# A mixture-of-experts kernel with seven-product blocks: the first groups reordered on ACT, PE and POOL

## The reference

```python
x = x + L0(x, probs, shared_gate)      # x: 16 x 256 tokens x 256, D = 256, F = 1024, f32

def L0(h, gating_probs, shared_gate_prob, Wg, Wu, Wd, Sg, Su, Sd):
    g = jnp.einsum('bsd,edf->ebsf', h, Wg)              # 8 experts
    u = jnp.einsum('bsd,edf->ebsf', h, Wu)
    expert_outs = jnp.einsum('ebsf,efd->ebsd', jax.nn.silu(g) * u, Wd)
    expert_output = jnp.einsum('be,ebsd->bsd', gating_probs, expert_outs)
    shared = jnp.einsum('bsf,fd->bsd', jax.nn.silu(h @ Sg) * (h @ Su), Sd)
    sg = shared_gate_prob[:, :, None]
    return (1.0 - sg) * expert_output + sg * shared
```

## Time and profile before

| | us |
|---|---|
| median of 3 runs | 2124.58 (2123.74 to 2124.72) |
| profiled execution, its own time | 2123.92 |
| its span, first to last instruction | 2122.1 |

### The profile page before, as it was taken

How to read it: one execution, slowest core, us unless ns; L and a number is a source line. 1 busy time by engine, 2 the same in 40 slices (tenths; PEclk the granted TensorE clock), 3 DMA queues, 4 the chain that set the end, 5 groups by cost and what they waited for, 6 DMA issues and landing times.

```text
span 2122.1 us, 33959 instructions
## 1 busy us (share of the span) xinstructions
PE 2098.0 (99%) x9180; PEld 1717.0 (81%) x9180; DVE 1452.6 (68%) x2640; ACT 1303.7 (61%) x2336; POOL 1609.4 (76%) x1435
## 2 busy tenths in 40 slices
PE   7999999999999999999999999999999999999998
PEld 5888888888788888888878888888887888888886
DVE  6666666666666666666676666666667666666666
ACT  6777777777556555555555655555555555555554
POOL 7988777878388777777778877777777777777776
PEclk9999999999999999999999999999999999999999
DMA  8776767666555455455445555445445555544543
GB/s 297 243 250 224 253 225 249 227 241 225 191 208 208 177 206 199 173 198 208 176 188 204 189 200 207 177 187 208 189 177 206 185 201 206 202 173 196 208 180 117
DMA packets 122455, 433.78 MB, mean 204 GB/s; under 512 B 13728, under 2 KB 41504, under 8 KB 122400
## 3 DMA queue, kind: packets, MB, share of 16 engines
q1 hardware_dynamic: 122400, 433.19, 54.5%
HBM read 329.85 MB, written 103.28 MB: 204 GB/s over the span
## 4 chain that ended last, share of the span: by engine, by line
PE 97%; DVE 1%; issue 0%; DMA 0%; POOL 0%; ACT 0%; SPq 0%; DVEq 0%; ACTq 0%; POOLq 0%
PE chain_ps L549 15%; PE chain_ps L551 14%; PE chain_ps L550 14%; PE down_ps L551 8%; PE down_ps L549 8%; PE down_ps L550 8%; PE p_ps L549 6%; PE p_ps L551 6%; PE p_ps L550 6%; PE side_ps L549 4%; PE side_ps L550 4%; PE side_ps L551 4%; DVE acc L972 1%; DMA w_raw<-w 0%; DVE h_forms L975 0%
## 5 line engine op out<-in xcount | busy, mean ns | idle before, releaser
L386 POOL TENSOR_TENSOR h_forms<-h_t,h_forms 128x512 fp32r<-128x512 f32 x432 | 564.3, 1325 | 274.2 <-ACT h_forms L858 274.2
L549 PE MATMUL chain_ps<-x_hi,gate_forms 128*128 128x512 f32 x1080 | 423.9, 393 | 2.2 <-DVE p_ps L972 1.1
L551 PE MATMUL chain_ps<-x_hi,gate_forms 128*128 128x512 f32 x1080 | 421.1, 390 | 0.0
L550 PE MATMUL chain_ps<-x_lo,gate_forms 128*128 128x512 f32 x1080 | 420.8, 390 | 0.0
L386 POOL TENSOR_TENSOR h_t<-h_b,h_t 128x512 f32<-128x512 f32 x214 | 312.6, 1461 | 78.9 <-DVE h_b L966 63.6
L972 DVE TENSOR_TENSOR p_ps<-tap_p,chain_ps 128x512 f32<-128x512 f32 x216 | 150.3, 696 | 251.5 <-PE chain_ps L551 251.5
L875 ACT COPY chain_ps<-chain_ps 128x512 f32<-128x512 f32 x216 | 123.1, 570 | 289.3 <-DVE h_a L966 201.3
L858 ACT CAST h_forms<-h_t 128x512 fp32r<-128x512 f32 x432 | 268.9, 623 | 14.9 <-DVE h_t L975 2.2
L386 POOL TENSOR_TENSOR w_lo<-w_raw,w_hi 128x1152 fp32r<-128x1152 f32 x71 | 190.5, 2683 | 85.7 <-ACT w_hi L775 84.8
L549 PEld LDWEIGHTS chain_ps<-x_hi,gate_forms 128*128 128x128 f32 x1080 | 202.5, 188 | 60.9 <-ACT chain_ps L875 8.1
L551 PEld LDWEIGHTS chain_ps<-x_hi,gate_forms 128*128 128x128 f32 x1080 | 202.7, 188 | 43.4
(11 more groups left out here) (105 smaller groups left out, 4882.2 us busy)
## 6 DMA issues: line engine op xcount, KB each, us to landing
...
```

Of the source, the lines that this page charges most:

```text
L386: return nc.gpsimd.tensor_tensor(dst, a, b, ALU.subtract)
L549: nc.tensor.matmul(bank, w_high, hi, start=start, stop=False, **on)
L550: nc.tensor.matmul(bank, w_high, lo, start=False, stop=False, **on)
L551: return nc.tensor.matmul(bank, w_low, hi, start=False, stop=stop, **on)
```

## The change

Four things. (1) ACT: in the first two units its work stands in the order in which it is needed; tap_p1(0) comes after the third x form. In units 2 to 7 it makes the high parts of chunks 3, 4, 5, 6 (and 7 behind the silus), 8, 9, and the down high parts of pairs 0, 1, 2, 3, 4 in units 2, 3, 5, 6, 7. (2) PE: in units 0 and 1 the plain products stand ahead of chained ones, and P4(0) behind P1 and P5 of chunk 1. (3) The second chunk's forms are made in parts on ACT and POOL, and POOL has a written order for its first eight units (`first_chunks`); keep(0), (2), (4), (6) of SP wait for the down sums too, since these now may come after the low parts. (4) The x forms of the next group start eight units later (OPENING_DELAY), and a fourth expert is written out on ACT and POOL. On DVE the low part of A11, A12 moves ahead of the sums, the x low parts are reordered, and gate0, gate1 of chunk 0 stand ahead of the last x low part.

```diff
@@ -29,6 +29,13 @@
 X_HI_AT = {6: B11, 8: T1, 10: B21, 12: T2, 14: B22, 16: T3, 18: T4}
 X_LO_AT = {10: B11, 12: T1, 14: B21, 16: T2, 18: B22, 20: T3, 22: T4}
 X_EXPERTS = 3
+OPENING_EXPERTS = 4
+OPENING_DELAY = 8
+
+HI_IN_UNIT = {2: 3, 3: 4, 4: 5, 5: 6, 6: 8, 7: 9}
+HI_BEHIND_UNIT = {5: 7}
+DOWN_HI_IN_UNIT = {2: 0, 3: 1, 5: 2, 6: 3, 7: 4}
+FIRST_X_HI = (B11, T1, B21, B22, T2, T3, T4)
 SUM_OF = {T1: 0, T2: 1, T3: 2, T4: 3}
 
 H_AT = {B11: 0, T1: 2, B22: 4, B21: 6, T2: 8, T3: 10, T4: 12}
...
@@ -263,6 +272,8 @@
             def keep(e, k):
                 n = group(0, e, k)
                 s, j = k % SLOTS, k // 2
+                if isinstance(n, int) and n in (0, 2, 4, 6):
+                    sp.wait_ge(d_sums, 4 * (j + 1))
                 if k % 2 == 1:
                     sp.wait_ge(d_lo_done, e * PAIRS + j + 1)
                 elif isinstance(n, int) and n == 0:
...
@@ -448,33 +459,71 @@
                 pool.wait_ge(x_hi_done, X_FORMS * g + form + 1)
                 subtract(x_lo[:, g % 2, form], x_source(g, form), x_hi[:, g % 2, form].bitcast(F32)).then_inc(x_lo_done, 1)
 
-            def next_x(g, e, k):
-                at = e * CHUNKS + k
+            def next_x(g, e, k, delay=0):
+                at = e * CHUNKS + k - delay
                 if g + 1 < GROUPS and at in X_SUM_AT:
                     x_form(g + 1, X_SUM_AT[at])
                 if g + 1 < GROUPS and at in X_LO_AT:
                     x_form_lo(g + 1, X_LO_AT[at])
 
...
+            def next_sums(e, k):
                 n = group(0, e, k)
                 s = (k + 1) % SLOTS
                 if not isinstance(n, int) or n < PER - 1:
                     uses = e * (CHUNKS // SLOTS) + (k + 1) // SLOTS + 1
                     pool.wait_ge(w_loaded[s], 16 * uses)
                     weight_sums(n + 1, s)
+
+            def pair_sums(e, k):
+                n = group(0, e, k)
+                uses = e * (CHUNKS // SLOTS) + k // SLOTS + 1
+                pool.wait_ge(d_loaded[k % SLOTS], 16 * uses)
+                pool.wait_ge(d_loaded[(k + 1) % SLOTS], 16 * uses)
+                if not isinstance(n, int) or n >= 4:
+                    pool.wait_ge(d_hi_done, e * PAIRS + k // 2 - 1)
+                down_sums(e * PAIRS + k // 2, k // 2)
+
+            def prepare(e, k):
+                next_sums(e, k)
                 if k % 2 == 0:
-                    uses = e * (CHUNKS // SLOTS) + k // SLOTS + 1
-                    pool.wait_ge(d_loaded[k % SLOTS], 16 * uses)
-                    pool.wait_ge(d_loaded[s], 16 * uses)
-                    if not isinstance(n, int) or n >= 4:
-                        pool.wait_ge(d_hi_done, e * PAIRS + k // 2 - 1)
-                    down_sums(e * PAIRS + k // 2, k // 2)
-                if not isinstance(n, int) or n > 0:
-                    weight_lo(e, k)
+                    pair_sums(e, k)
+                weight_lo(e, k)
                 if k % 2 == 1:
                     down_lo(e, k // 2)
-                if isinstance(e, int) and e < X_EXPERTS:
-                    next_x(0, e, k)
+                if isinstance(e, int) and e < OPENING_EXPERTS:
+                    next_x(0, e, k, OPENING_DELAY)
+
+            def second_lo(first, last):
+                return subtract(lo_of(1, first, last), raw_of(1, first, last), hi_of(1, first, last).bitcast(F32))
+
+            def first_chunks():
+
+                next_sums(0, 0)
+                pool.wait_ge(w1_hi_done, 1)
+                second_lo(A11, A12).then_inc(w1_lo_done, 1)
+                pool.wait_ge(w_hi_done, 1)
+                second_lo(S3, S4).then_inc(w1_lo_done, 1)
+                next_sums(0, 1)
+                pool.wait_ge(w_hi_done, 2)
+                second_lo(D0, D1).then_inc(w_lo_done, 1)
+                weight_lo(0, 2)
+                pair_sums(0, 0)
+                next_sums(0, 2)
+                down_lo(0, 0)
+                weight_lo(0, 3)
+                next_sums(0, 3)
+                pair_sums(0, 2)
+                weight_lo(0, 4)
+                down_lo(0, 1)
+                next_sums(0, 4)
+                pair_sums(0, 4)
+                next_sums(0, 5)
+                weight_lo(0, 5)
+                next_sums(0, 6)
+                down_lo(0, 2)
+                pair_sums(0, 6)
+                weight_lo(0, 6)
+                prepare(0, 7)
 
...
@@ -517,10 +566,11 @@
                     next_x(g, e, 2 * j + 1)
                 form_lo_of(T1, 5, pc + 1)
 
-            for e in range(X_EXPERTS):
+            first_chunks()
+            for e in range(1, OPENING_EXPERTS):
                 for k in range(CHUNKS):
                     prepare(e, k)
-            with pool.Fori(X_EXPERTS, EXPERTS - 1) as e:
+            with pool.Fori(OPENING_EXPERTS, EXPERTS - 1) as e:
                 for k in range(CHUNKS):
                     prepare(e, k)
             for k in range(CHUNKS):
...
+            def p1_of(n, k):
+                s = k % SLOTS
                 opening = isinstance(n, int) and n == 0
-                if not opening:
-                    p4(0, (k - 1) % CHUNKS, n - 1, first=isinstance(n, int) and n == 1)
                 if opening:
                     first_w(0)
+                elif isinstance(n, int) and n == 1:
+                    pe.wait_ge(w1_lo_done, 1)
                 else:
                     pe.wait_ge(w_lo_done, n)
                 after(pe, h_lo_done[0], n - 1)
-                product(chain, made(s, A11), x_of(0, B11, opening), start=True, stop=True).then_inc(p1_done, 1)
+                product(chain_ps[:, k % 2, :], made(s, A11), x_of(0, B11, opening), start=True, stop=True).then_inc(p1_done, 1)
+
...
+            def p6_of(n, k):
                 pe.wait_ge(p1_tapped, n + 1)
-                product(chain, made(s, S2), x_of(0, T2, opening), start=False, stop=True, goes_on=True).then_inc(p6_done, 1)
+                opening = isinstance(n, int) and n == 0
+                product(
+                    chain_ps[:, k % 2, :], made(k % SLOTS, S2), x_of(0, T2, opening), start=False, stop=True, goes_on=True
+                ).then_inc(p6_done, 1)
+
...
+            def first_units():
+
+                p1_of(0, 0)
+                p5_of(0, 0)
+                p2_of(0, 0)
+                p6_of(0, 0)
+                p3_of(0, 0)
+                p7_of(0, 0)
+                p1_of(1, 1)
+                p5_of(1, 1)
+                p4(0, 0, 0, first=True)
+                p6_of(1, 1)
+                p3_of(1, 1)
+                p2_of(1, 1)
+                p7_of(1, 1)
+                pe.wait_ge(h_lo_done[1], 1)
+                first_w(3)
+                down1(0, start=True, stop=False)
+
+            def unit(e, k):
+
+                n = group(0, e, k)
+                p4(0, (k - 1) % CHUNKS, n - 1)
+                p1_of(n, k)
+                p5_of(n, k)
+                pe.wait_ge(h_lo_done[0], n - 1)
+                down0((k - 2) % CHUNKS, start=isinstance(n, int) and n == 2, stop=False)
+                p6_of(n, k)
+                p2_of(n, k)
+                p3_of(n, k)
+                p7_of(n, k)
+                pe.wait_ge(h_lo_done[1], n)
+                down1((k - 1) % CHUNKS, start=False, stop=False)
 
             Q_OF = {1: (DA11, B11), 2: (DA12, B21), 3: (DS4, B22), 4: (DA22, T4), 5: (DS1, T1), 6: (DS2, T2), 7: (DS3, T3)}
             SUM_BANK = {2: q2_ps, 3: q3_ps, 4: q4_ps, 5: q5_ps}
...
-            for k in range(CHUNKS):
+            first_units()
+            for k in range(2, CHUNKS):
                 unit(0, k)
             with pe.Fori(1, EXPERTS) as e:
...
+            def silu_of(t, n):
+                act.wait_ge((gate0_done, gate1_done)[t], n + 1)
+                after(act, (h0_done, h1_done)[t], n)
+                nc.scalar.activation(silu[:, t], gate[:, t], ACT.Silu).then_inc(silu_done[t], 1)
+
+            def unit(e, k):
+                n = group(0, e, k)
+                early = isinstance(n, int) and n < CHUNKS
+                if early:
+                    chunk, behind, down_pair = HI_IN_UNIT[n], HI_BEHIND_UNIT.get(n), DOWN_HI_IN_UNIT.get(n)
+                    chunk = divmod(chunk, CHUNKS)
+                    down_pair = None if down_pair is None else divmod(down_pair, PAIRS)
+                else:
+                    chunk, behind = ahead_of(e, k), None
+                    if isinstance(n, int) and n + AHEAD >= PER:
+                        chunk = None
+                    down_pair = (chunk[0], chunk[1] // 2) if chunk and k % 2 == 1 else None
+
+                h1_hi_of(n - 1)
+                tap1(n, k)
+                tap5(n)
+                h0_hi_of(n - 1, k - 1)
+                if chunk:
+                    weight_hi(*chunk, 0)
+                tap_u2_of(n, k)
+                if chunk:
+                    weight_hi(*chunk, 1)
+                    if down_pair:
+                        down_hi(*down_pair)
+                if isinstance(e, int) and e < OPENING_EXPERTS:
+                    next_x(0, e, k, OPENING_DELAY)
```

(89 more changed lines are left out.)

80 lines of the change are left out of this document (28 added, 52 removed).

## The result

Over 20 runs each, the changed kernel takes 2127.66 us (median, 2124.9 to 2129.07), the kernel before 2124.36 us (2122.96 to 2126.68). The ratio is 1.0015 with an interval of 1.0008 to 1.0021: some 3 us slower, inside the 0.2% that the prediction called no change, and 1.6 us above the 2126.1 that it named. The profiled execution of the changed kernel has a span of 2124.6 us and took 2126.7 us.

A forecast was written before the change was run, and what follows sets the result against it. PE is busy 99% of the span, so only its idle time or slow-clock matmuls can be won. Opening gain 5.5 less loop loss 7.0 gives 1.5 us later: 2126.1 us, range 2125.4 to 2127.8, chance 0.58.

The forecast's parts named there:

- The opening: Up to P1 of chunk 2: the new order starts P1(2) at 24.0 instead of 29.52, a gain of 5.5 us.
- The POOL loops: Chunks 3 to 6: PE waits for POOL's w_lo, which waits on ACT's high parts; a loss of 7.0 us.
- the one behind chunk 6: After P1(6): no further stall, PE keeps 7.48 us a unit, the shift of 1.5 us stands to the end.
- (D): Opening wins less, through DVE contention 1 us and a late clock rise: 2127.1 to 2128.1 us; chance 0.13.
- (B): PE keeps the opening's whole gain because POOL leads by 3 to 5 us: 5.5 us faster, 2119.1; chance 0.10.
- (A): Loops cost less, chunk 6's loss is gone: 2.1 us faster, 2122.5; chance 0.13.
- (C): POOL's own steps lengthen in the loops beside DVE, from 13% more (2.8 us): 2128.9 us; chance 0.06.
- Edits at nothing: SP's later keeps and loads, longer ACT and POOL programs (0 to 0.3 us), second_lo in pieces: taken as no cost.
- the rule weighed: DVE and POOL contend for SBUF: x_lo of B22 and w_lo of S3, A22 could be charged 0.5 us in all.

The follow-up runs named there:

- e1: The changed kernel with ACT making the high parts of down pair 2 in unit 4 instead of unit 5; ratio to before 0.9990.
- e5: The changed kernel with only POOL's order in units 2 to 7 rewritten, same steps, each w_lo ahead of the d_lo; ratio to before 0.9979.
- e4: The changed kernel with 12 filler matmuls on PE in its pause ahead of P1 of chunk 6, output the same; ratio to before 1.0005.
- e6: The kernel before with only the x forms eight units later and a fourth expert written out; median 2124.04 us against 2124.24, ratio 0.9999.
- e9: e5 with SP's loads of w(n+4) ahead of the d form stores in the first eight chunks; median 2118.06 us, ratio to before 0.9971.

## Why the prediction was right, and where it was short

**The opening.** P1(0) 5.2 (5.25 measured), P5(0) 8.1 (8.23), P6(0) 11.1 (10.93), P1(2) 24.0 (23.66). The two pauses of PE before P2(1) and P4(1), 0.85 and 1.3 us, came as 1.0 and 0.9. The waits before these two ended with the steps named, DVE's h1_lo and up1. In between, errors cancelled: up1(0) came 0.6 us earlier than summed (14.82 for 15.4) and the coefficients behind it took 1.23 us for the 0.84, where the range had allowed for 0.17. The clock rose at 12.3, taken as 12.4; that this is so near is luck, since in the other traces with PE's same opening it rose between 11.2 and 12.9. P1(2) lay between 23.35 and 23.66 in all of them, so the reading that the moment hardly matters held.

**The POOL loops.** Chunk 3: loss 1.6, measured 1.68 (32.82 - 23.66 = 9.16 for 7.48). Chunk 4: 0, measured 0.17. Chunk 5: 1.8, measured 1.72. Chunk 6: 3.6, measured 3.55 (11.03 for 7.48). Sum 7.0, measured 7.1. P1(6) was put at 61.0 and came at 60.70, the waits of PE at 1.6, 1.7 and 3.5 and came as 1.5, 1.5 and 3.3. POOL idle for d_hi, 2.9 and 3.5, came as 2.75 and 3.6. e1 opened the last loop and e5 took away the waits of all of them but 0.15 us, so this cause is shown, not argued.

**The step that was short** is the one behind chunk 6: "No further stall [...] PE keeps the 7.48". There was no further stall, but PE did not keep the pace. The prediction worked out that PE would stand 3.5 us and, in another paragraph, what the clock costs in the opening, and did not put the two together. From P1(6) to P1(9) the trace has 23.92 us where three units take 22.44, 1.5 us. By the marks the change costs 1.3 + 1.5 = 2.7 us; the prediction had 1.5 + 0. e4 shows that the second term is the clock, but for some 0.1 us. With the measured 1.5 us added the forecast would have been 2127.6.

The Trainium skill ("TensorE: Matmul & The Clock Gate", Part 1) says that a TensorE that has idled goes back to the lower clock. This case's traces agree, with 0.57 granted behind a pause of 3.3 us; the fall in e6's trace, where no pause since the rise was longer than 1.3 us, is not covered by that sentence.

The median is 0.6 us above what the marks explain (3.3 for 2.7) with an interval of 1.7 to 4.5 us, so nothing is to be explained there. The time alone would not have told the forecast from rival (D), whose 2127.1 to 2128.1 take in the 2127.66 too; the marks do. Of the rivals, (B) had the right picture of what is to be had: e5 and e9 keep 4.5 and 5.5 us of the opening's gain, by the order of POOL (and in e9 of SP's loads) and not by POOL's old lead. (A) is what e1 made: 2.3 us faster at the marks for the 2.1 named, with no pause before P1(6) and no fall of the clock behind it. (C) did not come in the loops: POOL's w_lo and four sums take 2.61 to 2.69 and 1.84 us there, as in the earlier trace rows. It came in the opening, where PE waited for none of it: the first two pieces of second_lo took 2.96 us for 2.28. (D) did not come: the opening won 5.9 us for the 5.5 summed. "Edits at nothing": keep(0) at 24.35 (24.5), and the loads were hidden in the changed kernel. In e5, with PE 6 us further ahead, the cover of loads 5 and 7 was gone, which that paragraph had only for a load that is itself slow. The 0 to 0.3 us for the longer program rest on no row; e6 carries that edit too and shows no difference.

The contention of the rule weighed (0.5 us) did not appear as a loss in the changed kernel: x_lo of B22 took 0.88 us instead of 0.69, but w_lo of S3, A22 took 0.41 where it had taken 0.67, and P1(2) came 0.3 us earlier than summed. In e6's trace it may have been far larger (the 2.90 us).
